# Moving one subtraction per slot of an image-token front end from VectorE to GpSimd

## The chip, the core and the metric

One core of a Trainium2 chip runs the whole program. The metric is the device time of one execution in microseconds (us), the median of several runs. Beside it stands one profiled execution, whose trace gives the start and duration of every instruction on TensorE (PE, its weight loads PEld), VectorE (DVE), ScalarE (ACT), GpSimd (POOL) and the DMA queue of SyncE (SP).

## The reference

The input is 16 images of 3 x 112 x 112, cut into 784 patches of 16 x 16. Each patch goes through a small residual network and a projection to a token of 192 numbers:

```python
x = (x - mean) / (1e-06 + std)
x = x / math.sqrt(P)
x = _conv2d(x, conv1_w, conv1_b)
residual = x
x = _group_norm(x, gn1_g, gn1_b)
x = jax.nn.gelu(x, approximate=False)
x = _conv2d(x, rconv1_w, rconv1_b)
x = _group_norm(x, gn2_g, gn2_b)
x = jax.nn.gelu(x, approximate=False)          # the second activation
x = _conv2d(x, rconv2_w, rconv2_b)
x = residual + x
x = _conv2d(x, proj_w, proj_b, stride=P, pad=0)
```

Behind it come an attention block and an MLP branch over the 16 x 49 tokens. The change doesn't touch them; they are called the tail here.

## The kernel before, in words

**Precision.** TensorE multiplies in fp16, and the kernel keeps fp32 accuracy by splitting an fp32 value into a high fp16 part and a low fp16 part, low = value - high. The first activation is split by `split1` (a cast for the high part and a subtraction for the low one, both on VectorE). The second activation, the buffer `g2f`, has its high part made by ScalarE (`hi2`) and its low part by a subtraction (`split2`, L803 to L808). Both parts go to `arena` (named `g2` in the code), where a later group's projection reads them.

**Slots.** A unit is 8 patches, a slot is 4 patches (half a unit), and there are 98 units, so 196 slots. A group is 14 units, 28 slots; there are 7 groups. In slot k TensorE runs the 3x3 convolution of slot k (15 pairs of matmuls, L501 and L502), the small matmul `means` that averages statistics over the channels of a group-norm group (L544, behind the tenth pair), and the first convolution `conv1` four slots ahead (L535, L536, behind the thirteenth pair). In groups 1 to 6 it also weaves in the projection of the group before (L556, L560), in slots 4 to 27 of the group; group 0 and the first four slots of the others have none. The last group is projected behind the loop.

**VectorE in slot k** (`slot`, L811 to L827) goes strictly in this order: four statistics of a convolution result and four of a `conv1` result (L768, eight instructions that read PSUM), `moments` (L775, L776, L778, L780: 128 x 16 elements each), `split2` of slot k-3 (L808, 128 x 512 elements), `read_means` (L784, which waits for `means` of TensorE, then L787 and L789), and `split1` of slot k+2 (L799, L801).

**GpSimd in slot k** runs `norm` (L357 to L373): it waits for L789, raises 8 variances per partition to the power -0.5 (L363) and makes scale and shift with four more instructions of 8 elements, the last being L373. ScalarE waits for the shift, and does the two Gelus (`gelu1` L417, `gelu2` L425) and `hi2` (L433).

**What sets the order.** Each engine has a program of its own, written out by hand, with loops over pairs of units and over pairs of groups, and waits on semaphores between engines. An engine never passes a waiting instruction. The semaphore `s_sp2` counts `split2`; ScalarE waits for it before it overwrites half of `g2f`, TensorE before it projects a group, and VectorE at the end. `s_sp2h` counts `hi2`.

**DMA.** SyncE issues the transfers: per slot four copies of the first activation between halves of the partitions (L276), per unit two loads of patches (L256), and chunks of projection weights (L285).

Of the kernel before, what the change touches and what calls it, by code (L numbers as in the profile page):

```python
# [20 lines left out]
ALU, ACT = mybir.AluOpType, mybir.ActivationFunctionType  # L21
# [9 lines left out]
Q = 4  # L31
UNITS = NPAT // U
GU = 14
GROUPS = UNITS // GU
# [35 lines left out]
def build_front(nc, a, emb, xs, ts, wrd):  # L70
# [9 lines left out]
    with ExitStack() as ctx:  # L80
        def sb(name, shape, dt=F32):
            return ctx.enter_context(nc.sbuf_tensor("sb_" + name, shape, dt))

        def sem(name):
            return ctx.enter_context(nc.semaphore(name))
# [6 lines left out]
        g2 = arena[:, :, :].rearrange("p b (h g n) -> p b h g n", h=2, g=G)  # L92
# [5 lines left out]
        g2f = sb("g2f", [128, U, HALF])  # L98
# [80 lines left out]
        s_g2, s_sp2h, s_sp2 = sem("gelu2_done"), sem("split2_hi"), sem("split2_done")  # L179
        s_pc, s_pj, s_pjr, s_emb = sem("chunk_used"), sem("projected"), sem("tokens_out"), sem("emb_stored")  # L180
# [7 lines left out]
        def over_groups(eng, group):  # L188

            group(0, 0, True)  # L190
            with eng.Fori(0, (GROUPS - 1) // 2) as i:
                group(2 * i + 1, 1, False)
                group(2 * i + 2, 0, False)

        def slot2(j, p, q, old):

            return (2 * GU + 2 * p + q - 3) * Q if old else j * U * 2 + (2 * p + q - 3) * Q

        def over_units(eng, g, pair, first):

            pair(g * GU, 0, first)
            with eng.Fori(1, GU // 2) as j:
                pair(g * GU + 2 * j, j, False)
# [141 lines left out]
        @block.gpsimd  # L345
        def _(pool):
            gp = nc.gpsimd
            gp.memset(half_neg[:, :], -0.5).then_inc(s_cst, 1)
            gp.memset(half_pos[:, :], 0.5).then_inc(s_cst, 1)
            gp.memset(zeros[:, :], 0.0).then_inc(s_cst, 1)  # L350
            gp.memset(zt, 0.0).then_inc(s_zero, 1)
            gp.memset(xhl.bitcast(F32), 0.0).then_inc(s_xz, 1)
            pool.wait_ge(s_cst, 3)
            pool.wait_ge(s_xvar, 1)
            gp.tensor_tensor(xsd[:, 1, :], xsd[:, 0, :], half_pos[0:ROWS, :], ALU.pow).then_inc(s_xstd, 1)

            def norm(n, s, guard=True):  # L357

                ch = Chain(pool, s_pch, n * 4)
                mean, var, (t1, t2, t3) = mst[s][:, 0, :], mst[s][:, 1, :], (tmp[s][:, k, :] for k in range(3))  # L360
                bias, gam, bet = (wid[:, k, :] for k in range(3))
                pool.wait_ge(s_rd, n + 2)
                ch.did(gp.tensor_tensor(t1, var, half_neg[:, :], ALU.pow))  # L363
                ch.did(gp.tensor_tensor(t2, mean, bias, ALU.subtract))
                pool.wait_ge(s_pch, ch.at - 1)
                if guard:
                    pool.wait_ge(s_g1, n - 1)
                    pool.wait_ge(s_g2, n - 1)
                ch.did(gp.tensor_tensor(gsc[s][:, :], t1, gam, ALU.mult))
                ch.wait()  # L370
                ch.did(gp.tensor_tensor(t3, t2, gsc[s][:, :], ALU.mult))
                ch.wait()
                gp.tensor_tensor(gsh[s][:, :], bet, t3, ALU.subtract).then_inc(s_sh, 1)  # L373

            def pair(u0, j, first):
                for p in range(2):
                    for q in range(2):
                        norm(2 * (u0 + p) + q + 3, 1 - q)

            pool.wait_ge(s_padz, 3)  # L380
            norm(0, 0, False)
            norm(1, 1, False)
            norm(2, 0)
            over_groups(pool, lambda g, b, first: over_units(pool, g, pair, first))
            norm(2 * UNITS + 3, 1)

        @block.scalar
        def _(act):
# [263 lines left out]
        def _(dve):  # L652
            v = nc.vector
# [13 lines left out]
            for src, dst in ((fst32, fws), (tst32, tws), (w1st32, w1hl)):  # L667
                hi, lo = (dst[:, k].rearrange("p a b -> p (a b)") if len(dst.shape) == 4 else dst[:, k, :] for k in range(2))
# [59 lines left out]
            for q in range(6):  # L728
                c, pr = q // 2, q % 2
                src = xt[:, c].rearrange("p w (r k j) -> p w r k j", k=2, j=P)[:, :, :, pr, :]  # L730
# [34 lines left out]
            def channel_stats(s, src, at):  # L765

                for m in range(Q):
                    v.bn_stats(bn6[s][:, at + m, :], src[:, m * HALF:(m + 1) * HALF]).then_inc(s_dch, 1)  # L768

            def moments(n, s, n0):  # L770

                ch = Chain(dve, s_dch, n0)
                ch.wait()
                b6 = bn6[s][:, :, :].rearrange("p g (e k) -> p g e k", e=2)
                ch.did(v.tensor_tensor(ms[s][:, 0, :, :], b6[:, :, :, 1], wid2[:, :, :], ALU.add))  # L775
                ch.did(v.tensor_scalar(ms[s][:, 1, :, :], b6[:, :, :, 2], 2.0 / HALF, EPS * WS * WS, ALU.mult, ALU.add))  # L776
                dve.wait_ge(s_dch, ch.at - 1)
                ch.did(v.tensor_tensor(msq[s][:, :, :], ms[s][:, 0, :, :], ms[s][:, 0, :, :], ALU.mult))  # L778
                ch.wait()
                v.tensor_tensor(ms[s][:, 1, :, :], ms[s][:, 1, :, :], msq[s][:, :, :], ALU.add).then_inc(s_ms, 1)  # L780

            def read_means(n, s):
                dve.wait_ge(s_st, n + 1)
                v.tensor_reduce(mst[s][:, :, :], st[:, 0:4 * U].rearrange("p (a b k) -> p a b k", a=2, k=2),  # L784
                                mybir.AxisListType.X, ALU.add).then_inc(s_mv, 1)
                dve.wait_ge(s_mv, 2 * n + 1)
                v.tensor_tensor(msm[s][:, :], mst[s][:, 0, :], mst[s][:, 0, :], ALU.mult).then_inc(s_mv, 1)  # L787
                dve.wait_ge(s_mv, 2 * n + 2)
                v.tensor_tensor(mst[s][:, 1, :], mst[s][:, 1, :], msm[s][:, :], ALU.subtract).then_inc(s_rd, 1)  # L789
# [10 lines left out]
                dve.wait_ge(s_sp1h, k + 1)  # L800
                v.tensor_tensor(lo, src, hi, ALU.subtract).then_inc(s_sp1, 1)  # L801

            def split2(k, q, buf, slot):  # L803

                dve.wait_ge(s_sp2h, k + 1)
                src = g2f[:, q * Q:q * Q + Q, :]
                hi, lo = (g2[:, buf, h, bass.ds(slot, Q), :] for h in range(2))
                v.tensor_tensor(lo, src, hi, ALU.subtract).then_inc(s_sp2, 1)  # L808

            def group(g, b, first):  # L810
                def slot(u, q, p, j, head, first):  # L811

                    pair_at = g * (GU // 2) + j

                    k = 2 * u + q
                    seen = not (first and p == 0 and q == 0)
                    if seen:
                        dve.wait_ge(s_rc, k)
                        channel_stats(1 - q, rc[p][0] if q == 1 else rc[1 - p][1], Q)
                    dve.wait_ge(s_c1, k + 5)  # L820
                    channel_stats(1 - q, c1[1 - q], 0)
                    moments(k + 3, 1 - q, 11 * k + 25 if seen else 25)
                    if not (first and p == 0) and not (first and p == 1 and q == 0):
                        old = head and 2 * p + q < 3
                        split2(k - 3, 1 - q, 1 - b if old else b, slot2(j, p, q, old))
                    read_means(k + 3, 1 - q)
                    split1(k + 2, q, 1 - p, pair_at + 1)  # L827

                def pair(u0, j, first, head):
                    for p in range(2):  # L830
                        for q in range(2):
                            if head and p == 1 and q == 1:
                                dve.wait_ge(s_pj, g if not first else 1)
                            slot(u0 + p, q, p, j, head, first)

                pair(g * GU, 0, first, True)
                with dve.Fori(1, GU // 2) as j:
                    pair(g * GU + 2 * j, j, False, False)
# [32 lines left out]
            K = 2 * UNITS  # L871
# [3 lines left out]
            channel_stats(1, c1[1], 0)  # L875
            moments(K + 3, 1, 11 * K + 25)
            read_means(K + 3, 1)
            for k in (K - 3, K - 2, K - 1):
                split2(k, k % 2, 0, (2 * GU + k - K) * Q)

            dve.wait_ge(s_pj, GROUPS)
            dve.wait_ge(s_sp1, K + 2)
            dve.wait_ge(s_sp2, K + 2)
# [3 lines left out]
            for c in range(C):  # L887
                for m in (2 * c, 2 * c + 1):
                    dve.wait_ge(s_tc[m % NTC], 32 * (m // NTC + 1))
                for ky in range(3):  # L890
                    for kx in range(3):
                        for py in range(2):
# [3 lines left out]
                            lo, hi = max(0, kx - 1), min(P, P + kx - 1)  # L896
# [696 lines left out]
```

## Time and profile before

| | |
|---|---|
| Device time, median of 3 runs | 1586.49 us (1581.76 to 1587.44) |
| The profiled execution | 1585.12 us, of which the span from first to last instruction is 1583.3 us |
| Granted TensorE clock, mean over the span | 0.963 |
| PE busy | 1429.4 us (90%) |
| DVE busy | 1134.6 us (72%) |
| ACT busy | 837.4 us (53%) |
| POOL busy | 581.8 us (37%) |
| The slots of the loop | from about 252 us to 1256 us of the span |

The table averages over a set-up of some 250 us, the loop and a tail of some 300 us. The limit of a stretch is read from that stretch alone: the distance between one row of a kind and the next of the same kind gives the length of a slot. A row of the timeline has the start, the duration, the engine, the line and the operation; rows of one kind that follow each other are merged, with their count.

### The profile page before, as it was taken

How to read it: one execution, taken by the hardware profiler on the slowest of the kernel's cores; microseconds unless marked ns; L12 is line 12 of the kernel's file. 1: busy time of each engine (PE TensorE's matmuls, PEld its weight loads, DVE VectorE, ACT ScalarE, POOL GpSimd, SP SyncE). 2: the span in 40 equal slices, each digit the busy share in tenths (PEclk: the TensorE clock that was granted, in tenths of full speed). 3: DMA queues.
4: the chain of work that ended last, by engine and by line, in shares of the span. 5: the costliest groups of instructions: out<-in, count | busy, mean ns of one | idle time of the engine just before them, and what ended most of it. 6: DMA issues, size and time to landing. Idle time of an engine off the chain costs nothing. (4 is left out here: it accounts for less than half of the span.)

```text
span 1583.3 us, 42709 instructions
## 1 busy us (share of the span) xinstructions
PE 1429.4 (90%) x13490; PEld 1008.6 (64%) x13490; DVE 1134.6 (72%) x4227; ACT 837.4 (53%) x2102; POOL 581.8 (37%) x1111
## 2 busy tenths in 40 slices
PE   6969996888999999989999998999999766978889
PEld 2424442333688588858877875888588666655647
DVE  7723334999988888888888887888888750474710
ACT  1212222777777676766767666666767501333442
POOL 2000003555544455444454544445554401161500
PEclk9989997999999999999999999999999887987999
DMA  6463325433555455445545553554555577300000
GB/s 181 122 205 88 99 87 220 100 101 101 138 148 143 123 150 143 131 121 145 144 119 151 146 140 101 149 147 128 139 144 143 160 202 167 71 1 1 2 3 14
DMA packets 117219, 190.63 MB, mean 120 GB/s; under 512 B 18252, under 2 KB 86284, under 8 KB 116942
## 3 DMA queue, kind: packets, MB, share of 16 engines
q1 hardware_dynamic: 117070, 188.60, 43.6%
q8 instruction: 99, 1.62, 0.4%
q14 instruction: 50, 0.41, 0.1%
HBM read 103.34 MB, written 21.30 MB: 79 GB/s over the span
## 5 line engine op out<-in xcount | busy, mean ns | idle before, releaser
L363 POOL TENSOR_TENSOR sb_tmp<-sb_mst,sb_half_neg 128x8 f32<-128x8 f32 x200 | 354.6, 1773 | 684.4 <-DVE sb_mst L789 684.4
L501 PE MATMUL rc<-sb_acts,sb_rwd 128*64 128x512 f16 x1764 | 563.5, 392 | 18.3 <-DMA sb_acts<-sb_hst 18.2
L502 PE MATMUL rc<-sb_acts,sb_rwd 128*64 128x512 f16 x1764 | 564.7, 393 | 0.0
L417 ACT ACTIVATE sb_f32q<-c,sb_gsh,sb_gsc 128x128 f32<-128x128 f32 x792 | 298.2, 458 | 285.6 <-POOL sb_gsh L373 285.6
L501 PE MATMUL rc<-sb_acts,sb_rwl 128*64 128x512 f16 x1176 | 363.9, 391 | 5.2 <-issue 5.2
L502 PE MATMUL rc<-sb_acts,sb_rwl 128*64 128x512 f16 x1176 | 363.4, 391 | 0.0
L556 PE MATMUL pj<-sb_wall,sb_arena 128*64 128x384 f16 x1792 | 309.9, 337 | 21.7 <-DMA sb_wall<-w_lo 15.1
L425 ACT ACTIVATE sb_g2f<-rc,sb_gsh,sb_gsc 128x128 f32<-128x128 f32 x784 | 297.3, 481 | 4.4 <-POOL sb_gsh L373 4.4
L560 PEld LDWEIGHTS pj<-sb_wall,sb_arena 128*64 128x64 f16 x1792 | 219.0, 222 | 63.8
L560 PE MATMUL pj<-sb_wall,sb_arena 128*64 128x192 f16 x1792 | 240.9, 247 | 0.0
L556 PEld LDWEIGHTS pj<-sb_wall,sb_arena 128*64 128x64 f16 x1792 | 215.5, 219 | 38.8 <-DMA sb_wall<-w_lo 16.4
L501 PEld LDWEIGHTS rc<-sb_acts,sb_rwd 128*64 128x64 f16 x1764 | 180.1, 110 | 79.6 <-DMA sb_acts<-sb_hst 28.4
L476 PE MATMUL rc<-sb_acts,sb_arena 128*128 128x512 f16 x864 | 196.7, 386 | 29.9 <-DVE sb_acts L684 29.9
L502 PEld LDWEIGHTS rc<-sb_acts,sb_rwd 128*64 128x64 f16 x1764 | 180.2, 110 | 4.9
L768 DVE BATCH_NORM_STATS2 sb_bn<-rc 128x6 f32<-128x128 f32 x784 | 174.0, 285 | 12.0 <-issue 5.7
L768 DVE BATCH_NORM_STATS2 sb_bn<-c 128x6 f32<-128x128 f32 x800 | 175.1, 282 | 0.5 <-PE c L536 0.5
L476 PEld LDWEIGHTS rc<-sb_acts,sb_arena 128*128 128x128 f16 x864 | 82.0, 97 | 136.2 <-issue 35.5
L501 PEld LDWEIGHTS rc<-sb_acts,sb_rwl 128*64 128x64 f16 x1176 | 126.7, 109 | 47.1 <-issue 9.6
L808 DVE TENSOR_TENSOR sb_arena<-sb_g2f,sb_arena 128x512 f32 (+1 forms) x196 | 135.7, 693 | 28.7 <-issue 18.0
L801 DVE TENSOR_TENSOR sb_acts<-sb_f32q,sb_hst 128x512 f16<-128x512 f32 x198 | 137.8, 696 | 6.8
L433 ACT ACTIVATE sb_arena<-sb_g2f 128x512 f32 (+1 forms) x196 | 124.9, 637 | 26.0 <-ACT sb_g2f L425 8.6
L502 PEld LDWEIGHTS rc<-sb_acts,sb_rwl 128*64 128x64 f16 x1176 | 126.9, 109 | 0.4 <-issue 0.3
(158 smaller groups left out, 1726.2 us busy)
## 6 DMA issues: line engine op xcount, KB each, us to landing
sb_acts<-sb_hst SPq DMA_DIRECT2D x792, 78.8 KB, 2.6
sb_wall<-w_lo SPq DMA_DIRECT2D x56, 528.0 KB, 3.8
sb_im<-x_planes SPq DMA_DIRECT2D x202, 136.5 KB
sb_wall<-w_lo SPq DMA_DIRECT2D x28, 480.0 KB, 3.7
sb_f32q<-in_proj SPq DMA_DIRECT2D x12, 576.0 KB, 3.9
sb_arena<-in_proj SPq DMA_DIRECT2D x12, 576.0 KB, 4.4
w_lo<-sb_arena SPq DMA_DIRECT2D x1, 6144.0 KB, 17.3
scratch_fold<-sb_wall SPq DMA_DIRECT2D x48, 123.8 KB
```

The source lines that it names most:

```text
L363: ch.did(gp.tensor_tensor(t1, var, half_neg[:, :], ALU.pow))
L417: ins = nc.scalar.activation(g1f[:, q * Q + m, :], c1[q][:, m * HALF:(m + 1) * HALF], ACT.Gelu, bias=gsh[q][:, m:m + 1], scale=gsc[q][:, m ...
L425: ins = nc.scalar.activation(g2f[:, q * Q + m, :], rc[p][q][:, m * HALF:(m + 1) * HALF], ACT.Gelu, bias=gsh[q][:, Q + m:Q + m + 1], scale= ...
L433: nc.scalar.activation(g2[:, buf, 0, bass.ds(slot, Q), :], g2f[:, q * Q:q * Q + Q, :], ACT.Copy).then_inc(s_sp2h, 1)
L476: last = nc.tensor.matmul(out, w[:, wp, 3 * t + m, :], v[:, xp, t:t + 8, m * Q:(m + P) * Q], start=(n == 0), stop=(n == 17))
L501: nc.tensor.matmul(out[0:CH, :], w_odd, x_odd, start=(n == 0), stop=(n == 14))
L502: yield nc.tensor.matmul(out[CH:128, :], w_even, x_even, start=(n == 0), stop=(n == 14))
L556: last = nc.tensor.matmul(pj[at:at + 64, 0:2 * E], g2[:, b, 0, k:k + 64, n], both, start=(n == 0), stop=False)
L560: last = nc.tensor.matmul(pj[at:at + 64, 0:E], g2[:, b, 1, k:k + 64, n], whi[:, n, :], start=False, stop=(n == HALF - 1))
L768: v.bn_stats(bn6[s][:, at + m, :], src[:, m * HALF:(m + 1) * HALF]).then_inc(s_dch, 1)
L801: v.tensor_tensor(lo, src, hi, ALU.subtract).then_inc(s_sp1, 1)
L808: v.tensor_tensor(lo, src, hi, ALU.subtract).then_inc(s_sp2, 1)
```

## The change

The subtraction `split2` leaves VectorE's program, where it stood between `moments` and `read_means`, and joins GpSimd's, behind `norm` of the same slot. Operands and types are the same. The wait on `s_sp2h` goes with it, and so does the wait on `s_pj` in the fourth slot of each group, which keeps a half of `arena` from being overwritten before it was projected. The last three subtractions, behind the loop, move to GpSimd too. The numbering of the semaphores stays.

```diff
-            def pair(u0, j, first):
-                for p in range(2):
-                    for q in range(2):
-                        norm(2 * (u0 + p) + q + 3, 1 - q)
+            def split2(k, q, buf, slot):
+                pool.wait_ge(s_sp2h, k + 1)
+                src = g2f[:, q * Q:q * Q + Q, :]
+                hi, lo = (g2[:, buf, h, bass.ds(slot, Q), :] for h in range(2))
+                gp.tensor_tensor(lo, src, hi, ALU.subtract).then_inc(s_sp2, 1)
+
+            def group(g, b, first):
+                def pair(u0, j, first, head):
+                    for p in range(2):
+                        for q in range(2):
+                            k = 2 * (u0 + p) + q
+                            norm(k + 3, 1 - q)
+                            if head and p == 1 and q == 1:
+                                pool.wait_ge(s_pj, g if not first else 1)
+                            if not (first and p == 0) and not (first and p == 1 and q == 0):
+                                old = head and 2 * p + q < 3
+                                split2(k - 3, 1 - q, 1 - b if old else b, slot2(j, p, q, old))
...
             norm(2 * UNITS + 3, 1)
+            for k in range(2 * UNITS - 3, 2 * UNITS):
+                split2(k, k % 2, 0, (2 * GU + k - 2 * UNITS) * Q)
...
-            def split2(k, q, buf, slot):
-
-                dve.wait_ge(s_sp2h, k + 1)
-                src = g2f[:, q * Q:q * Q + Q, :]
-                hi, lo = (g2[:, buf, h, bass.ds(slot, Q), :] for h in range(2))
-                v.tensor_tensor(lo, src, hi, ALU.subtract).then_inc(s_sp2, 1)
...
                     moments(k + 3, 1 - q, 11 * k + 25 if seen else 25)
-                    if not (first and p == 0) and not (first and p == 1 and q == 0):
-                        old = head and 2 * p + q < 3
-                        split2(k - 3, 1 - q, 1 - b if old else b, slot2(j, p, q, old))
                     read_means(k + 3, 1 - q)
                     split1(k + 2, q, 1 - p, pair_at + 1)
...
-                            if head and p == 1 and q == 1:
-                                dve.wait_ge(s_pj, g if not first else 1)
...
-            for k in (K - 3, K - 2, K - 1):
-                split2(k, k % 2, 0, (2 * GU + k - K) * Q)
```

VectorE, one slot in the body of the loop over pairs of units, from the first instruction of `moments` on, before (`sb_arena` is where the low part goes, `st` the result of `means` in PSUM; ISA and REGISTER_ALU are waits and address arithmetic):

```order
L775 TENSOR_TENSOR sb_ms<-sb_bn_0,sb_wid 128x16
L776 TENSOR_SCALAR sb_ms<-sb_bn_0 128x16
L777 REGISTER_ALU
L778 TENSOR_TENSOR sb_msq<-sb_ms 128x16
L67 REGISTER_ALU
L780 TENSOR_TENSOR sb_ms<-sb_ms,sb_msq 128x16
L805 REGISTER_ALU
L808 ISA
L808 REGISTER_ALU
L808 TENSOR_TENSOR sb_arena<-sb_g2f,sb_arena 128x512
L784 TENSOR_REDUCE sb_mst<-st 128x16
```

The same slot of the changed kernel, where the lines 775 to 784 have become 797 to 806:

```order
L797 TENSOR_TENSOR sb_ms<-sb_bn_0,sb_wid 128x16
L798 TENSOR_SCALAR sb_ms<-sb_bn_0 128x16
L799 REGISTER_ALU
L800 TENSOR_TENSOR sb_msq<-sb_ms 128x16
L67 REGISTER_ALU
L802 TENSOR_TENSOR sb_ms<-sb_ms,sb_msq 128x16
L806 TENSOR_REDUCE sb_mst<-st 128x16
```

The subtraction and its address arithmetic are gone, and the reduction that waits for TensorE's `means` stands directly behind the last instruction of `moments`.

GpSimd, one slot of the same loop, before:

```order
L363 TENSOR_TENSOR sb_tmp<-sb_mst,sb_half_neg 128x8
L364 TENSOR_TENSOR sb_tmp<-sb_mst,sb_wid 128x8
L365 ISA
L369 TENSOR_TENSOR sb_gsc<-sb_tmp,sb_wid 128x8
L67 REGISTER_ALU
L371 TENSOR_TENSOR sb_tmp<-sb_tmp,sb_gsc 128x8
L67 REGISTER_ALU
L373 TENSOR_TENSOR sb_gsh<-sb_wid,sb_tmp 128x8
L362 ISA
```

The same slot of the changed kernel:

```order
L363 TENSOR_TENSOR sb_tmp<-sb_mst,sb_half_neg 128x8
L364 TENSOR_TENSOR sb_tmp<-sb_mst,sb_wid 128x8
L365 ISA
L369 TENSOR_TENSOR sb_gsc<-sb_tmp,sb_wid 128x8
L67 REGISTER_ALU
L371 TENSOR_TENSOR sb_tmp<-sb_tmp,sb_gsc 128x8
L67 REGISTER_ALU
L373 TENSOR_TENSOR sb_gsh<-sb_wid,sb_tmp 128x8
L376 REGISTER_ALU
L379 ISA
L379 REGISTER_ALU
L379 TENSOR_TENSOR sb_arena<-sb_g2f,sb_arena 128x512
```

The subtraction, now L379, follows the shift L373 with its wait and its address arithmetic ahead of it; the next slot's wait for L789 comes behind it.

## Rows read from the trace of the kernel before

**Rows 1.** The profile's page: busy time of the engines over the whole span.

```profile
PE 1429.4 (90%) x13490; PEld 1008.6 (64%) x13490; DVE 1134.6 (72%) x4227; ACT 837.4 (53%) x2102; POOL 581.8 (37%) x1111
```

**Rows 2.** Line 789 in two stretches: count, duration (min/median/max), first and last start.

```profile
L789 DVE TENSOR_TENSOR sb_mst<-sb_mst,sb_msm x21: 166/167/170, 288.1 to 380.7; 128x8 f32<-128x8 f32 x21
...
L789 DVE TENSOR_TENSOR sb_mst<-sb_mst,sb_msm x22: 166/166/168, 412.6 to 519.3; 128x8 f32<-128x8 f32 x22
```

**Rows 3.** Stretches: length, then busy PE, PEld, DVE, ACT, POOL, clock, DMA.

```profile
288.00:385.00 97.00, 86.29 (x756) 36.34 (x756) 90.50 (x378) 73.68 (x189) 52.77 (x105) 1.00 0.40 101
410.00:522.00 112.00, 110.86 (x1256) 94.25 (x1254) 99.07 (x402) 78.20 (x199) 56.20 (x114) 1.00 0.54 146
```

**Rows 4.** Waits from 288 to 385 us: total, times, longest.

```profile
PEld st L544 <- DVE sb_ms L780: 17.8, 20, 1.0
```

**Rows 5.** Timeline of VectorE, one slot of group 0.

```profile
339.00 0.17 DVE L789 TENSOR_TENSOR sb_mst<-sb_mst,sb_msm 128x8 f32<-128x8 f32 x1
...
341.86 0.17 DVE L775 TENSOR_TENSOR sb_ms<-sb_bn,sb_wid 128x16 f32<-128x16 f32 x1
...
342.07 0.18 DVE L778 TENSOR_TENSOR sb_msq<-sb_ms 128x16 f32<-128x16 f32 x1
342.28 0.18 DVE L780 TENSOR_TENSOR sb_ms<-sb_ms,sb_msq 128x16 f32<-128x16 f32 x1
342.63 0.69 DVE L808 TENSOR_TENSOR sb_arena<-sb_g2f,sb_arena 128x512 f32 x1 [0.17 <-issue]
343.24 0.18 DVE L784 TENSOR_REDUCE sb_mst<-st 128x16 f32<-128x32 f32 x1
...
343.66 0.17 DVE L789 TENSOR_TENSOR sb_mst<-sb_mst,sb_msm 128x8 f32<-128x8 f32 x1
```

**Rows 6.** Timeline of GpSimd in the same slot, and the last step of the next.

```profile
340.97 0.20 POOL L364 TENSOR_TENSOR sb_tmp<-sb_mst,sb_wid 128x8 f32<-128x8 f32 x1
341.13 0.20 POOL L369 TENSOR_TENSOR sb_gsc<-sb_tmp,sb_wid 128x8 f32<-128x8 f32 x1
...
341.68 0.20 POOL L373 TENSOR_TENSOR sb_gsh<-sb_wid,sb_tmp 128x8 f32<-128x8 f32 x1
...
346.47 0.20 POOL L373 TENSOR_TENSOR sb_gsh<-sb_wid,sb_tmp 128x8 f32<-128x8 f32 x1
```

**Rows 7.** Timeline of VectorE behind the last slot, where no subtraction stands between.

```profile
1254.68 0.17 DVE L780 TENSOR_TENSOR sb_ms<-sb_ms,sb_msq 128x16 f32<-128x16 f32 x1
1255.27 0.19 DVE L784 TENSOR_REDUCE sb_mst<-st 128x16 f32<-128x32 f32 x1 [0.41 <-PE st L544]
1255.50 0.17 DVE L787 TENSOR_TENSOR sb_msm<-sb_mst 128x8 f32<-128x8 f32 x1
1255.70 0.17 DVE L789 TENSOR_TENSOR sb_mst<-sb_mst,sb_msm 128x8 f32<-128x8 f32 x1
```

**Rows 8.** Timeline of a slot with projection: GpSimd, then VectorE.

```profile
706.56 0.20 POOL L373 TENSOR_TENSOR sb_gsh<-sb_wid,sb_tmp 128x8 f32<-128x8 f32 x1
...
706.86 0.18 DVE L778 TENSOR_TENSOR sb_msq<-sb_ms 128x16 f32<-128x16 f32 x1
707.07 0.17 DVE L780 TENSOR_TENSOR sb_ms<-sb_ms,sb_msq 128x16 f32<-128x16 f32 x1
```

**Rows 9.** Timelines of VectorE and GpSimd where their instructions overlap, or don't.

```profile
257.61 0.69 DVE L801 TENSOR_TENSOR sb_acts<-sb_f32q,sb_hst 128x512 f16<-128x512 f32 x1
...
257.71 0.65 POOL L371 TENSOR_TENSOR sb_tmp<-sb_tmp,sb_gsc 128x8 f32<-128x8 f32 x1
...
1406.29 0.84 DVE L1433 TENSOR_TENSOR tl_pr<-tl_pr,tl_mx 128x294 f32<-128x294 f32 x2
...
1417.27 1.36 DVE L1433 TENSOR_TENSOR tl_pr<-tl_pr,tl_mx 128x294 f32<-128x294 f32 x2
...
1416.61 1.32 POOL L1071 TENSOR_TENSOR tl_kb<-tl_big,tl_hmask 96x294 f32<-96x294 f32 x2
```

**Rows 10.** GpSimd on two tensors of 294 elements, in the tail: duration min/median/max.

```profile
L1071 POOL TENSOR_TENSOR tl_kb<-tl_big,tl_hmask x64: 672/678/905, 1384.9 to 1496.1; 96x294 f32<-96x294 f32 x64
```

**Rows 11.** SyncE's queue of transfers in group 0.

```profile
341.96 1.56 SPq L256 DMA_DIRECT2D sb_im<-x_planes  x2
344.23 7.03 SPq L276 DMA_DIRECT2D sb_acts<-sb_hst  x8
```

More of the change, by code:

```diff
@@ L373, in norm @@
                 gp.tensor_tensor(gsh[s][:, :], bet, t3, ALU.subtract).then_inc(s_sh, 1)
-            def pair(u0, j, first):
-                for p in range(2):
-                    for q in range(2):
-                        norm(2 * (u0 + p) + q + 3, 1 - q)
+            def split2(k, q, buf, slot):
[14 more added lines that the diff above has]
+                                split2(k - 3, 1 - q, 1 - b if old else b, slot2(j, p, q, old))
+                pair(g * GU, 0, first, True)
+                with pool.Fori(1, GU // 2) as j:
+                    pair(g * GU + 2 * j, j, False, False)
             pool.wait_ge(s_padz, 3)
@@ L383, in _ @@
             norm(2, 0)
-            over_groups(pool, lambda g, b, first: over_units(pool, g, pair, first))
+            group(0, 0, True)
+            with pool.Fori(0, (GROUPS - 1) // 2) as i:
+                group(2 * i + 1, 1, False)
+                group(2 * i + 2, 0, False)
             norm(2 * UNITS + 3, 1)
+            for k in range(2 * UNITS - 3, 2 * UNITS):
+                split2(k, k % 2, 0, (2 * GU + k - 2 * UNITS) * Q)
         @block.scalar
```

## The prediction

> **What bounds the kernel now.** The page comes first, and it misleads: PE is busy for 90% of the span, VectorE for 72%, GpSimd for 37% [rows 1]. That reads as if GpSimd had plenty of room for one more subtraction. Shares over the span mix a set-up, a loop and a tail, and the change touches the loop alone, so I went on to the length of a slot there. L789 comes once in each slot. In group 0, which has no projection, 21 of them start between 288.1 and 380.7 us: 92.6 over 20 intervals, 4.63 us a slot. With projection, 22 start between 412.6 and 519.3: 106.7 over 21, 5.08 us a slot [rows 2]. Two kinds of slot, and the busy time of the stretches tells their limits: with projection PE is busy for 110.86 of 112 us; without it for 86.29 of 97, and it waits for VectorE's L780, 20 times, 17.8 us by the weight loads [rows 3, 4]. The third view is VectorE's timeline in such a plain slot: its instructions follow each other without a hole from one L789 to the next [rows 5] (starts overlap by some 0.1 us, so that 90.50 busy of 97 is a full engine). So plain slots are bound by VectorE's order, slots with projection by PE, and GpSimd idles in both.
>
> **What the change removes.** VectorE loses the 0.69 us subtraction L808 in each slot, but not all of its time is won. Before, L780 ends at 342.28 + 0.18 = 342.46 and L784 starts at 343.24, 0.78 us later [rows 5]. L784 needs TensorE's `means`, which needs L780; the subtraction lay over that round trip. Where nothing stands between, behind the last slot, L780 ends at 1254.85 and L784 starts at 1255.27, having waited for PE: 0.42 us [rows 7]. So the removal is worth 0.78 - 0.42 = 0.36 us in a plain slot, and nothing in a slot that PE bounds.
>
> **What it adds on GpSimd.** 196 subtractions of 128 x 512. No row has GpSimd at this size, so bounds: L1071 takes 0.678 us for 294 elements [rows 10], an instruction of 8 elements 0.20 [rows 6]. A straight line through both gives 0.20 + 0.478 x 504 / 286 = 1.04 us, simple proportion 0.678 x 512 / 294 = 1.18. I take 1.12, the middle; the two differ little. Its input is ready: the high part of slot k-3 is made a whole slot before GpSimd gets there, so the moved wait costs nothing, and neither does that on `s_pj`, whose projection ended at least three slots before. Queued behind the subtraction on GpSimd is only the next `norm`, which waits for the next L789. That leaves it room: L373 starts 2.68 or 2.81 us behind L789 (341.68 - 339.00, 346.47 - 343.66) [rows 5, 6], mean 2.75; with dispatch and 1.12 the engine is free before 4.3. No transfer is moved. ScalarE, which waits for `s_sp2` before it refills half of `g2f`, does a Gelu of its own first. By throughput the change is free.
>
> **What it costs: a collision.** VectorE and GpSimd get in each other's way here, and rows of this trace price it. VectorE's pair of L1433, each reading two tensors in SBUF, takes 0.84 us when GpSimd is quiet; started at 1417.27, while GpSimd's L1071 runs until 1416.61 + 1.32 = 1417.93, the pair takes 1.36: 0.52 longer, which is what was left of GpSimd's instruction (0.66) less some 0.14 [rows 9]. It goes the other way too: L371 of GpSimd, 0.20 us elsewhere, takes 0.65 when it starts under L801 and ends just behind it (257.71 + 0.65 = 258.36 against 258.30) [rows 9]. An instruction that reads SBUF on the one engine holds off one that reads two SBUF tensors on the other until it ends.
>
> Now lay the new subtraction on the timeline. It starts behind L373 by its dispatch: 0.16 us from L364 to L369, where a wait stands between (341.13 - 340.97) [rows 6], or 0.35 from L780 to L808, where address arithmetic and a wait do (342.63 - 342.28) [rows 5]. The order shows both on GpSimd now, so 0.35: it starts at 342.03. VectorE's L778 is due at 342.07 and L780 at 342.28 [rows 5]; in a slot with projection L373 starts at 706.56, the subtraction would at 706.91, L778 is due at 706.86 and L780 at 707.07 [rows 8]. So GpSimd gets in ahead of L780, and often of L778. Both read two SBUF tensors. They wait for its end, `means` waits for L780, L784 for `means`, L789 for L784, and GpSimd's next `norm` for L789: the wait closes a ring of its own. From L789 to the next L789:
>
> - to L373: 2.75; dispatch 0.35; subtraction 1.12;
> - release to the end of L780: 0.03 (its 0.18 less the 0.15 seen above);
> - L780 to L784: 0.42 [rows 7]; L784 to L789: 0.43 (1255.70 - 1255.27) [rows 7].
>
> That is 5.10 us if L780 alone is caught. If L778 is, L780 starts 0.21 behind it (342.28 - 342.07) [rows 5]: 5.31. It is nearly a tie between them, so I take the mean, 5.20 us for every slot. This is above VectorE's 4.63 and above PE's 5.08.
>
> The sum: 25 plain slots of group 0 at 5.20 - 4.63 = 0.57 give 14 us. 144 slots with projection (6 groups x 24) at 5.20 - 5.08 = 0.12 give 17. The 24 slots at the heads of groups 1 to 6 have waits of their own mixed in; I count half of a plain one's loss, an estimate: 7. Behind the loop the last three subtractions stand behind the last `norm`, and the last Gelu needs the half of `g2f` that the first of them frees: 1.12, and the last is longer by 1.12 - 0.69: 1.6 us. Together 40. The profiled execution took 1585.1 us (span 1583.3), 1.4 below the median of the runs: 1585 + 40 = 1625 us. With L780 alone caught, 12 + 6 + 3 + 2 = 22, 1607 us; with L778 always, 17 + 8 + 33 + 2 = 60, 1645 us; with the bounds of the subtraction's price some 4 to 10 us further out on either side. So 1600 to 1655 for this case by itself.
>
> The Trainium skill, SBUF — State Buffer, section Who interferes with whom, says that a VectorE instruction with two SBUF inputs contends with a GpSimd instruction that reads SBUF, and that whoever starts first keeps the shared ports for the whole instruction while the other is fully blocked. The rows above agree, but for 0.14 us of VectorE's start that the block hides. By the page alone each slot would be longer by that much, 0.15 us, and the sum 1652 instead of 1625.
>
> **The rivals.** *GpSimd comes too late.* If dispatch takes over 0.51 to 0.60 us (707.07 - 706.56, 342.28 - 341.68) [rows 5, 6, 8], L780 gets in first. It starts 3.28 behind L789, ends at 3.46, the subtraction runs from there to 4.58 and catches L787, due at 3.46 + 0.42 + 0.23 = 4.11 (L787 starts 0.23 behind L784 [rows 7]). That is held to about 4.43, and L789 comes at 4.63: the plain slot as before, PE's slot as before, and the end's 1.6 us: 1587. For it: the margin is 0.2 us, less than dispatch is known to.
>
> *No collision for small reads.* VectorE's instructions of 16 elements might slip through. Then plain slots gain 0.36, down to 4.27, but SyncE issues 7.03 + 1.56 us of transfers in two slots, 4.30 each [rows 11]: 0.33 x 25 = 8 us, 4 at the heads, and at best the 1% that PE idles with projection (1.14 of 112 [rows 3]), 7 of 731 us. Less 1.6, 1567 us, on the other side of no change. It decides if L780 ends less than 0.78 - 0.42 = 0.36 us later than it does now. Against it: GpSimd's block in rows 9 came for an instruction of 8 elements.
>
> *A dearer subtraction.* If mixed fp32 and fp16 operands cost GpSimd 1.6 us, each slot gains another 0.48: 1712 us or so. Nothing speaks for it but that no row has these types on GpSimd.
>
> **How the numbers follow.** The collision gets 0.60, GpSimd too late 0.18, no collision 0.12, the dearer subtraction 0.10. I forecast the likeliest, 1625 us. The range goes from 1570, just above the full gain, to 1668, above the page's case; outside it lie most of the dear case and a few of the hundredths of the gain. A measurement of this kernel tells 0.5% (8 us) from no change. Collision and dear price are slower by more: 0.70. Too late is the same: 0.18. No collision is faster: 0.12.
>
> **What would show it.** In the changed kernel's trace: GpSimd's subtraction at 1.04 to 1.18 us, starting 0.3 to 0.4 behind the shift; VectorE's second or third product of `moments` (128 x 16, 0.18 before) stretched to about 1 us in most slots; L789's successor every 5.1 to 5.3 us in all groups alike; PE waiting for `moments` with projection too, where it hardly did. Wrong would be: those instructions still at 0.18, or a subtraction that starts behind them, or one of over 1.3 us. Plain slots of 4.3 us would be the second rival.

## The result, and the profile after

The changed kernel takes 1643.59 us (median of 4 runs, 1640.66 to 1644.95), the kernel before 1584.85 us in the same comparison (median of 4, 1581.76 to 1587.44): 1.0369 times as long, 95% interval 1.0343 to 1.0395. Slower, as forecast, by 59 us where 40 were forecast; the time lies inside the range of 1570 to 1668.

Its page answers to [rows 1]:

```profile
PE 1454.5 (89%) x13490; PEld 984.6 (60%) x13490; DVE 1174.1 (72%) x4031; ACT 838.8 (51%) x2102; POOL 810.2 (49%) x1307
```

VectorE lost 196 instructions of 0.69 us, 135 us in all, and is busy for 40 us *more* than before. That is the first sign: its other instructions have become longer. The line that closes a slot, now L811, shows where the time went. First over the whole run, in the kernel before and then in the one after (count, duration min/median/max, first and last start):

```profile
L789 DVE TENSOR_TENSOR sb_mst<-sb_mst,sb_msm x200: 166/166/173, 252.7 to 1255.7; 128x8 f32<-128x8 f32 x100
```

```profile
L811 DVE TENSOR_TENSOR sb_mst<-sb_mst,sb_msm x200: 166/166/176, 252.7 to 1312.1; 128x8 f32<-128x8 f32 x100
```

The set-up ends at the same time, 252.7. The loop has grown from 1003.0 to 1059.4, by 56.4 us; the span has grown by 1641.7 - 1583.3 = 58.4, so 2.0 remain for what stands behind the loop. The same line in group 0 and in group 1, which answers to [rows 2]:

```profile
L811 DVE TENSOR_TENSOR sb_mst<-sb_mst,sb_msm x19: 166/166/169, 304.5 to 398.0; 128x8 f32<-128x8 f32 x19
...
L811 DVE TENSOR_TENSOR sb_mst<-sb_mst,sb_msm x21: 166/166/174, 429.4 to 536.1; 128x8 f32<-128x8 f32 x21
```

A plain slot takes 93.5 / 18 = 5.19 us (4.63 before), a slot with projection 106.7 / 20 = 5.33 (5.08 before). The busy times and the waits of these stretches, for [rows 3, 4]:

```profile
300.00:399.00 99.00, 75.04 (x692) 35.87 (x689) 87.94 (x324) 67.14 (x172) 70.28 (x115) 1.00 0.35 90
425.00:540.00 115.00, 111.83 (x1221) 86.52 (x1218) 101.71 (x369) 75.77 (x193) 80.39 (x132) 1.00 0.50 136
```

```profile
PEld st L566 <- DVE sb_ms L802: 33.2, 19, 1.9
...
PEld st L566 <- DVE sb_ms L802: 9.2, 21, 1.8
```

The first wait is that of group 0: 33.2 us in 19 slots where there were 17.8 in 20. The second is from the slots with projection: TensorE, which bounded them, now waits there for `moments` as well, 9.2 us by the weight loads in 115. In the kernel before, the same wait from 410 to 522 us was this:

```profile
PEld st L544 <- DVE sb_ms L780: 0.8, 1, 0.8
```

In both kinds of slot it is now a ring of waits that sets the length, and no engine by itself. VectorE and then GpSimd in one plain slot, for [rows 5, 6]:

```profile
351.30 0.17 DVE L811 TENSOR_TENSOR sb_mst<-sb_mst,sb_msm 128x8 f32<-128x8 f32 x1
...
354.40 0.17 DVE L800 TENSOR_TENSOR sb_msq<-sb_ms 128x16 f32<-128x16 f32 x1
354.61 1.01 DVE L802 TENSOR_TENSOR sb_ms<-sb_ms,sb_msq 128x16 f32<-128x16 f32 x1
356.03 0.19 DVE L806 TENSOR_REDUCE sb_mst<-st 128x16 f32<-128x32 f32 x1 [0.41 <-PE st L566]
...
356.46 0.17 DVE L811 TENSOR_TENSOR sb_mst<-sb_mst,sb_msm 128x8 f32<-128x8 f32 x1
```

```profile
354.11 0.20 POOL L373 TENSOR_TENSOR sb_gsh<-sb_wid,sb_tmp 128x8 f32<-128x8 f32 x1
354.41 1.18 POOL L379 TENSOR_TENSOR sb_arena<-sb_g2f,sb_arena 128x512 f32 x1
```

The whole ring is to be read off: 2.81 us from L811 to the shift, 0.30 to the subtraction, 1.18 for it until 355.59, 0.03 to the end of L802 at 355.62, 0.41 for TensorE's `means`, 0.43 to the next L811. That makes 5.16. The last product of `moments`, 0.18 us by itself, was issued 0.2 us behind the subtraction and lasted until its end.

A slot with projection looks like this on VectorE, then on GpSimd, and at the end of a convolution on TensorE:

```profile
482.72 0.17 DVE L811 TENSOR_TENSOR sb_mst<-sb_mst,sb_msm 128x8 f32<-128x8 f32 x1
...
483.26 0.69 DVE L823 TENSOR_TENSOR sb_acts<-sb_f32q,sb_hst 128x512 f16<-128x512 f32 x1
484.07 0.89 DVE L790 BATCH_NORM_STATS2 sb_bn<-rc 128x6 f32<-128x128 f32 x4
...
485.78 1.12 DVE L797 TENSOR_TENSOR sb_ms<-sb_bn,sb_wid 128x16 f32<-128x16 f32 x1
...
488.16 0.17 DVE L811 TENSOR_TENSOR sb_mst<-sb_mst,sb_msm 128x8 f32<-128x8 f32 x1
```

```profile
485.41 0.20 POOL L373 TENSOR_TENSOR sb_gsh<-sb_wid,sb_tmp 128x8 f32<-128x8 f32 x1
485.69 1.17 POOL L379 TENSOR_TENSOR sb_arena<-sb_g2f,sb_arena 128x512 f32 x1
```

```profile
483.65 0.38 PE L524 MATMUL rc<-sb_acts,sb_rwd 128*64 128x512 f16 x1
```

Here the statistics L790 begin 0.81 us behind L823 (352.48 - 351.87 = 0.61 in the plain slot), since the convolution that they read isn't ready sooner: its last matmul ends at 484.03 as the profile models it, 0.04 us ahead of L790. `moments` is later by the same 0.2 us, and the subtraction gets in ahead of its *first* instruction. The other three follow only then, and the slot is 5.44 us long. The four lines of `moments` and the subtraction over the whole run:

```profile
L797 DVE TENSOR_TENSOR sb_ms<-sb_bn,sb_wid x200: 174/179/1187, 250.3 to 1310.5; 128x16 f32<-128x16 f32 x100
...
L798 DVE TENSOR_SCALAR sb_ms<-sb_bn x200: 152/166/1193, 250.4 to 1310.8; 128x16 f32<-128x16 f32 x100
...
L800 DVE TENSOR_TENSOR sb_msq<-sb_ms x200: 159/175/1211, 250.5 to 1310.9; 128x16 f32<-128x16 f32 x100
...
L802 DVE TENSOR_TENSOR sb_ms<-sb_ms,sb_msq x200: 174/175/1161, 250.8 to 1311.1; 128x16 f32<-128x16 f32 x100
...
L379 POOL TENSOR_TENSOR sb_arena<-sb_g2f,sb_arena x196: 1151/1178/1245, 286.4 to 1318.3; 128x512 f32 x168, 128x512 f16<-128x512 f32 x28
```

All medians are below 0.2 us and all maxima at 1.2: in a slot one of the four is caught, and not always the same. A group's mean or median would hide this; the maximum and the timeline show it. Counted in the timeline by which of the four lasted over 0.45 us:

| Caught | Group 0, 300 to 399 us: slots, mean length | 425 to 1300 us: slots, mean length |
|---|---|---|
| L797, the first | 0 | 59, 5.42 |
| L798, the second | 5, 5.21 | 17, 5.30 |
| L800, the third | 6, 5.24 | 32, 5.32 |
| L802, the fourth | 7, 5.15 | 48, 5.21 |

The longer stretch holds the four heads, without projection, of groups 2 to 6 as well, and six of its 162 slots have none of that length. Between 425 and 1300 us the statistics begin 0.78 us behind L823 on average in the 59 slots of the first row, 0.62 to 0.64 in the other rows.

### The profile page after: what moved, and what is told of

Same layout as the page of the kernel before. It is cut to its first block and busy times, and to the rows that moved or that the text cites. A ratio compares the mean times of both kernels' runs of the same rounds, so it can differ in the third digit from the quotient of the medians.

```text
span 1641.7 us, 42709 instructions
## 1 busy us (share of the span) xinstructions
PE 1454.5 (89%) x13490; PEld 984.6 (60%) x13490; DVE 1174.1 (72%) x4031; ACT 838.8 (51%) x2102; POOL 810.2 (49%) x1307
## 5 line engine op out<-in xcount | busy, mean ns | idle before, releaser
L578 PE MATMUL pj<-sb_wall,sb_arena 128*64 128x384 f16 x1792 | 300.6, 337 | 20.7 <-DMA sb_wall<-w_lo 12.8
L582 PEld LDWEIGHTS pj<-sb_wall,sb_arena 128*64 128x64 f16 x1792 | 212.3, 226 | 74.0
L379 POOL TENSOR_TENSOR sb_arena<-sb_g2f,sb_arena 128x512 f32 (+1 forms) x196 | 231.7, 1183 | 16.1 <-issue 2.9
L578 PEld LDWEIGHTS pj<-sb_wall,sb_arena 128*64 128x64 f16 x1792 | 209.3, 222 | 40.7 <-DMA sb_wall<-w_lo 14.4
L582 PE MATMUL pj<-sb_wall,sb_arena 128*64 128x192 f16 x1792 | 231.3, 247 | 0.0
L790 DVE BATCH_NORM_STATS2 sb_bn<-rc 128x6 f32<-128x128 f32 x784 | 173.7, 283 | 11.5 <-issue 5.5
L790 DVE BATCH_NORM_STATS2 sb_bn<-c 128x6 f32<-128x128 f32 x800 | 174.3, 278 | 0.5 <-PE c L558 0.5
L523 PEld LDWEIGHTS rc<-sb_acts,sb_rwl 128*64 128x64 f16 x1176 | 126.6, 109 | 49.2 <-issue 7.7
L823 DVE TENSOR_TENSOR sb_acts<-sb_f32q,sb_hst 128x512 f16<-128x512 f32 x198 | 137.9, 696 | 6.8
L566 PE MATMUL st<-sb_ms,sb_grp 128*64 128x32 f32 x800 | 62.1, 234 | 74.0 <-DVE sb_ms L802 63.1
```

Of the source, the lines that this page charges most:

```text
L379: gp.tensor_tensor(lo, src, hi, ALU.subtract).then_inc(s_sp2, 1)
L523: nc.tensor.matmul(out[0:CH, :], w_odd, x_odd, start=(n == 0), stop=(n == 14))
L578: last = nc.tensor.matmul(pj[at:at + 64, 0:2 * E], g2[:, b, 0, k:k + 64, n], both, start=(n == 0), stop=False)
L582: last = nc.tensor.matmul(pj[at:at + 64, 0:E], g2[:, b, 1, k:k + 64, n], whi[:, n, :], start=False, stop=(n == HALF - 1))
```

## The experiments

Six kernels beside the two. Each is compared with the kernel before on the same chip (1586.0 us, for the last two 1585.56).

**1. The ceiling.** The kernel before, and VectorE's subtraction is left out: the low part of the second activation is not formed, and memory that is then written by nothing is zeroed once in the set-up. What is left is the most that any place for the subtraction could give.

```diff
-                v.tensor_tensor(lo, src, hi, ALU.subtract).then_inc(s_sp2, 1)
+                v.sem_inc(s_sp2, 1)
```

> The kernel before, with the subtraction left out on VectorE and put nowhere else (the low part of the second activation is never formed; its semaphore is still counted there; 1 us of zeroing is added ahead of the loop). This prices the removal alone. Collision theory: removing is worth something, plain slots 4.27 to 4.35 us instead of 4.63, slots with projection 5.05 to 5.08, time 1567 to 1576 us. Rival (the move loses because VectorE now waits for TensorE's means with nothing to cover the round trip): 1585 us or more.

Measured: 1581.69 us, 0.9974 times (0.9957 to 0.9991). The end of a slot (now L795) over the whole run, in plain slots, and with projection, then SyncE's queue in group 0:

```profile
L795 DVE TENSOR_TENSOR sb_mst<-sb_mst,sb_msm x200: 166/166/175, 256.9 to 1254.7; 128x8 f32<-128x8 f32 x100
...
L795 DVE TENSOR_TENSOR sb_mst<-sb_mst,sb_msm x19: 166/166/168, 301.5 to 381.6; 128x8 f32<-128x8 f32 x19
...
L795 DVE TENSOR_TENSOR sb_mst<-sb_mst,sb_msm x19: 166/166/168, 426.5 to 517.4; 128x8 f32<-128x8 f32 x19
```

```profile
335.80 1.56 SPq L257 DMA_DIRECT2D sb_im<-x_planes  x2
337.80 6.94 SPq L277 DMA_DIRECT2D sb_acts<-sb_hst  x8
344.78 1.56 SPq L257 DMA_DIRECT2D sb_im<-x_planes  x2
```

A plain slot takes 80.1 / 18 = 4.45 us, not 4.3, and a slot with projection 90.9 / 18 = 5.05. So the expectation missed: without 135 us of VectorE's work the time is 4 us shorter. Not all of the difference is the subtraction's: the loop starts at 256.9 us here and at 251.6 to 253.2 in the six profiles without the zeroing (252.7 in the kernel before), so that some 4 us of the experiment's time are its own set-up. The loop itself takes 1254.7 - 256.9 = 997.8 us for 1003.0. Less that set-up the time would be about 1577 us, an estimate, and the work is worth some 8 us, 0.5%. SyncE issues for 8.50 us of the 8.98 between its two rows of L257, two slots; what closes the rest of that ring wasn't taken apart. With the rest of the kernel as it is, no place for the subtraction can gain more than about this 0.5%.

**2. The collision alone.** The kernel before keeps its subtraction on VectorE; GpSimd gets one more of the same size behind each `norm`, on fp16 constants, and nothing waits for it.

```diff
                         norm(2 * (u0 + p) + q + 3, 1 - q)
+                        gp.tensor_tensor(junk[:, :], rwl[:, 0:8, :].rearrange("p a b -> p (a b)"),
+                                         rwd[:, 0:8, :].rearrange("p a b -> p (a b)"), ALU.subtract)
```

> The kernel before, subtraction left on VectorE, and on GpSimd behind each norm a further 128x512 subtraction of two constant weight tensors in SBUF into an unused tensor, which nobody waits for. This adds the collision alone, without moving any dependence. Collision theory: an instruction of moments is stretched by about 1 us in nearly every slot, the ring is 2.75 + 0.3 + 1.18 + 0.03 + 0.78 + 0.43 = 5.47 us, time 1650 to 1680 us. Rival (the move loses by the changed order of waits: what waits for the subtraction gets it later): 1585 to 1590 us.

Measured: 1701.16 us, 1.0741 times (1.0717 to 1.0766). Slots are 78.4 / 14 = 5.60 us without projection and 89.7 / 16 = 5.61 with it. One slot, GpSimd and then VectorE:

```profile
343.46 0.20 POOL L374 TENSOR_TENSOR sb_gsh<-sb_wid,sb_tmp 128x8 f32<-128x8 f32 x1
343.62 1.15 POOL L380 TENSOR_TENSOR sb_junk<-sb_rwl,sb_rwd 128x512 f16<-128x512 f16 x1
```

```profile
343.64 1.16 DVE L778 TENSOR_TENSOR sb_ms<-sb_bn,sb_wid 128x16 f32<-128x16 f32 x1
344.73 0.16 DVE L779 TENSOR_SCALAR sb_ms<-sb_bn 128x16 f32<-128x16 f32 x1
...
345.38 0.69 DVE L811 TENSOR_TENSOR sb_arena<-sb_g2f,sb_arena 128x512 f32 x1 [0.16 <-issue]
```

Work that no one waits for, in time in which its engine was idle, costs 115 us. That is the collision by itself. It is larger than expected for a reason that these rows show too: this subtraction has fixed addresses and no wait, starts 0.16 us behind the shift rather than 0.30, and so catches the first instruction of `moments` more often (for over 0.45 us in 101 slots of the whole run, 61 in the changed kernel), and then all four come later; the fourth is never caught in this run. When the block comes decides its price as much as how long it is.

**3. A write in place of a read.** The same place in the kernel before, but GpSimd only writes: a memset of 128 x 780 fp16, 0.75 us.

```diff
                         norm(2 * (u0 + p) + q + 3, 1 - q)
+                        gp.memset(junk[:, :], 0.0)
```

> The kernel before, and on GpSimd behind each norm a memset of 128x780 fp16 into an unused tensor, about 0.72 us, at the place of the further subtraction of extra_read. It occupies GpSimd and reads nothing. Collision through reads: no instruction of moments is stretched, 1583 to 1590 us. Rival (any GpSimd instruction holds VectorE off, or a longer GpSimd program is what costs): the ring is 2.75 + 0.3 + 0.72 + 0.03 + 0.78 + 0.43 = 5.01 us in plain slots, 1595 to 1605 us.

Measured: 1600.26 us, 1.0103 times (1.0076 to 1.013). The time is the rival's, but the rows tell another story than either: GpSimd, then VectorE.

```profile
345.74 0.75 POOL L380 MEMSET sb_junk<- 128x780 f16 x1
```

```profile
345.78 0.17 DVE L777 TENSOR_TENSOR sb_ms<-sb_bn,sb_wid 128x16 f32<-128x16 f32 x1
345.87 0.65 DVE L778 TENSOR_SCALAR sb_ms<-sb_bn 128x16 f32<-128x16 f32 x1
345.99 0.53 DVE L780 TENSOR_TENSOR sb_msq<-sb_ms 128x16 f32<-128x16 f32 x1
346.57 0.17 DVE L782 TENSOR_TENSOR sb_ms<-sb_ms,sb_msq 128x16 f32<-128x16 f32 x1
...
L777 DVE TENSOR_TENSOR sb_ms<-sb_bn,sb_wid x200: 174/176/205, 250.0 to 1265.7; 128x16 f32<-128x16 f32 x100
...
L778 DVE TENSOR_SCALAR sb_ms<-sb_bn x200: 165/650/756, 250.0 to 1265.8; 128x16 f32<-128x16 f32 x100
```

L777, with two tensors in SBUF, is never held (0.205 us at most in 200), though the memset is running when it starts in 97 of them; L778, with one, is held until the memset ends. L780 stands behind it on VectorE: in the five slots in which L778 started ahead of the memset and L780 under it (the first at 311.5 us), L780 took 0.17 us. So what holds the two-tensor instructions is that GpSimd *reads*, as the prediction had it; but a `tensor_scalar` is held by a GpSimd instruction that reads nothing, which the prediction had left out. The Trainium skill, SBUF — State Buffer, section Who interferes with whom, says both: two SBUF inputs contend only with a GpSimd instruction that reads SBUF, while `tensor_scalar` can enter a mode that takes the shared ports for itself and so contends with any. This trace agrees, with 0.17 us for L777 and 0.65 for L778; that L778 ran in such a mode is not itself seen in it.

**4. Another moment.** The changed kernel, with the subtraction held until the next slot's `moments` is done.

```diff
                 pool.wait_ge(s_sp2h, k + 1)
+                pool.wait_ge(s_ms, min(k + 8, 2 * UNITS + 4) if isinstance(k, int) else k + 8)
```

> The changed kernel with one more wait on GpSimd: the subtraction starts only when VectorE's moments of the next slot are done. Same instructions, same work, a later start. Collision theory: moments are at 0.17 us each again, the second instruction of read_means is held instead by 0.2 to 0.5 us, plain slots 4.6 to 4.7 us, 1583 to 1595 us. Rival (GpSimd is simply too slow for this subtraction, or its later result is what is waited for): 1640 us or more, since the result comes later still.

Measured: 1597.84 us, 1.0088 times (1.0055 to 1.0122); of the changed kernel's 3.7% some 0.9% are left, and `moments` is never held. But the block has moved on. VectorE, then GpSimd, in group 0:

```profile
340.45 0.17 DVE L803 TENSOR_TENSOR sb_ms<-sb_ms,sb_msq 128x16 f32<-128x16 f32 x1
341.04 0.19 DVE L807 TENSOR_REDUCE sb_mst<-st 128x16 f32<-128x32 f32 x1 [0.41 <-PE st L567]
341.26 0.89 DVE L810 TENSOR_TENSOR sb_msm<-sb_mst 128x8 f32<-128x8 f32 x1
```

```profile
340.97 1.16 POOL L380 TENSOR_TENSOR sb_arena<-sb_g2f,sb_arena 128x512 f32 x1 [0.81 <-DVE sb_ms L803]
```

The subtraction starts 0.35 us after the end of the instruction that it waited for (340.62 to 340.97), so that little of its 1.16 us lies under the round trip of `means`, which is over at 341.04. L807, which reads PSUM, passes; L810, which reads SBUF twice, is held until 342.15. Plain slots take 80.0 / 16 = 5.00 us, slots with projection 91.5 / 18 = 5.08, as in the kernel before. My expectation was a little too low, since it had the subtraction start at once.

**5. Half the length.** The changed kernel, with GpSimd forming only the first two of each slot's four patches (the rest of the low part is zero, from a memset in the set-up).

```diff
-                gp.tensor_tensor(lo, src, hi, ALU.subtract).then_inc(s_sp2, 1)
+                gp.tensor_tensor(lo[:, 0:2, :], src[:, 0:2, :], hi[:, 0:2, :], ALU.subtract).then_inc(s_sp2, 1)
```

> The changed kernel with half of the subtraction: GpSimd forms the low part for 2 of the 4 patches of each slot (128x256 elements), the other half is never formed; 1 us of zeroing is added ahead of the loop. Collision theory: the block is as long as what is left of GpSimd's instruction, so about 0.68 us instead of 1.18, the ring 0.5 us shorter: 4.6 to 5.0 us by which instruction is caught, mean 4.8 in plain slots, slots with projection back at PE's 5.08; 1587 to 1598 us. Rival (the move costs by its order of waits, whatever the length): 1625 us or more.

Measured: 1594.86 us, 1.0049 times (1.003 to 1.0068). The instruction, by the page (busy us, then mean ns), and the longest that any line of `moments` took, here its third:

```profile
L383 POOL TENSOR_TENSOR sb_arena<-sb_g2f,sb_arena 128x256 f32 (+1 forms) x196 | 133.6, 682 | 15.0 <-ACT sb_arena L459 1.7
```

```profile
L806 DVE TENSOR_TENSOR sb_msq<-sb_ms x200: 159/176/720, 254.2 to 1263.9; 128x16 f32<-128x16 f32 x100
```

The held instruction is as long as the shorter block, 0.72 us at most, and plain slots fall to 80.6 / 17 = 4.74 us, slots with projection to 91.3 / 18 = 5.07. Half the block costs 0.5% rather than 3.7%, and some 4 of these 9 us are again the zeroing in the set-up (the first L817 starts at 256.4 us). With projection nothing is lost: where the ring of waits isn't longer than what bounds the slot, the block costs no time.

**6. The same work in four pieces.** The changed kernel, with the whole subtraction as four instructions of 128 x 128.

```diff
-                hi, lo = (g2[:, buf, h, bass.ds(slot, Q), :] for h in range(2))
-                gp.tensor_tensor(lo, src, hi, ALU.subtract).then_inc(s_sp2, 1)
+                for m in range(Q):
+                    hi, lo = (g2[:, buf, h, bass.ds(slot + m, 1), :] for h in range(2))
+                    ins = gp.tensor_tensor(lo, src[:, m:m + 1, :], hi, ALU.subtract)
+                ins.then_inc(s_sp2, 1)
```

> The changed kernel with the same subtraction cut into four instructions of 128x128 elements on GpSimd, back to back, about 0.4 us from one to the next. Collision theory: VectorE gets in between two of them, each of its instructions on two SBUF tensors waits for the end of one quarter only, ring 4.8 to 5.15 us, 1592 to 1615 us although GpSimd is busy longer (1.6 us). Rival (what counts is when the whole subtraction ends, or how busy GpSimd is): 1660 us or more, since it ends 0.4 us later.

Measured: 1589.89 us, 1.0027 times (1.001 to 1.0044). GpSimd and VectorE in one slot, then the page's row of the pieces:

```profile
342.98 1.60 POOL L380 TENSOR_TENSOR sb_arena<-sb_g2f,sb_arena 128x128 f32 x4
```

```profile
343.04 0.40 DVE L800 TENSOR_SCALAR sb_ms<-sb_bn 128x16 f32<-128x16 f32 x1
343.36 0.17 DVE L802 TENSOR_TENSOR sb_msq<-sb_ms 128x16 f32<-128x16 f32 x1
343.56 0.29 DVE L804 TENSOR_TENSOR sb_ms<-sb_ms,sb_msq 128x16 f32<-128x16 f32 x1
...
L380 POOL TENSOR_TENSOR sb_arena<-sb_g2f,sb_arena 128x128 f32 (+1 forms) x784 | 316.3, 433 | 13.4 <-ACT sb_arena L457 0.8
```

GpSimd now works 1.60 us per slot for what took it 1.18, and yet the ratio falls from 1.0369 to 1.0027, a little below what was expected. Plain slots take 79.0 / 17 = 4.65 us, slots with projection 91.0 / 18 = 5.06. VectorE's short instructions get in between two pieces. Of the two readings of the slow-down, that GpSimd has too much to do or that one long instruction holds VectorE off, only the second survives this. It is still no gain over the kernel before, where the first experiment leaves room for 0.5% at most.

## Why the prediction was right, and where its sizes were off

**The mechanism is shown.** The work added alone, with nothing waiting for it, makes the loss (experiment 2); moving it off `moments` (4), halving it (5) or cutting it up (6) removes most of it. Of the rivals, GpSimd too late (1587) and no collision (1567) fall by the rows of L797 to L802, and the dearer subtraction by L379's 1.18 us, which is the upper bound that the prediction gave for 1.12. Dispatch was 0.30 us in the plain slot shown and 0.22 to 0.32 in 150 of the 196 slots, for 0.35. The end of the held instruction, 0.03 us behind the release, was as taken. The case by the Trainium skill alone had 0.15 us more per slot, and 1652; the measured time is nearer to that than to 1625, but not for its reason: in the rows above the 0.15 us are hidden.

**The terms of the sum.** Plain slots: 25 x (5.19 - 4.63) = 14 us, forecast 14. That they agree so well is partly chance: the shorter dispatch and the longer subtraction, 0.05 and 0.06 us, cancel, and the second instruction is caught there too. Behind the loop 2.0 us for 1.6, which says little: that stretch is 327.6 us in the kernel before and 329.7 in experiment 3, which ends in the same way. Slots with projection: the 144 of them take 764.6 us from L811 to L811, and 730.7 from L789 to L789 before, 34 us more (5.31 a slot for 5.07), forecast 17. The heads of groups 1 to 6, summed in the same way, take 9 us more, forecast 7. The mis-sized term is that of the projection, and the step is "I take the mean, 5.20 us for every slot": it allowed only L778 or L780 of the old numbering to be caught, the third and the fourth, with 5.31 as its longest. Measured between 425 and 1300 us, the first is caught in 59 of 156 slots, at 5.42, and the second in 17. Two things had been left out. `moments` comes later there against GpSimd's chain, because the statistics wait for TensorE, which is the busy engine in those slots: in 47 of the 53 slots with projection in which the first is caught, they begin 0.80 us or a little more behind L823, and 0.04 behind the end of the convolution's last matmul. And the second instruction, a `tensor_scalar` with one SBUF tensor, was taken as one that can't be held. That it can be is seen in the table above and, without any GpSimd read, in experiment 3.

**The removal.** Worth "0.36 us in a plain slot" by the round trip; experiment 1 has 4.63 - 4.45 = 0.18. This didn't enter the sum, since the collision overrides it, but the rival that ends on the other side was priced with it: without any subtraction the kernel takes 1581.69 us, some 1577 less the added set-up, so 1567 could not have been reached even with no collision.

## What to carry to other kernels

An idle engine isn't a free one: before moving work from VectorE to GpSimd, lay the new instruction on the timeline and look which VectorE instructions on the ring of waits read SBUF while it runs, since even one of 16 elements is held to its end. If the work has to be there, cut it into several short instructions, or put it under instructions that read PSUM (seen for L807 of experiment 4 alone, and not tried for a whole subtraction), and allow for the start behind a wait (0.35 us here). And time the kernel with the work left out first: here that shows that 135 us of busy time was worth some 8, and the set-up that such a run adds has to be taken off.

## What the runs showed of the hardware that was not expected

A GpSimd memset, which reads nothing, holds a `tensor_scalar` of 128 x 16 on VectorE for as long as it runs (0.65 us in the median for 0.17), and doesn't hold a `tensor_tensor` with two SBUF inputs beside it (0.176). GpSimd's subtraction takes 1.18 us for 512 elements, 0.68 for 256 and 0.43 for 128, which lies on a line of 0.18 us and 1.95 ns an element (worked out from the three); four of the shortest in a row take 1.60, 0.13 less than four times 0.43, since their rows overlap (the next starts about 0.39 us behind the last). A subtraction of 512 elements starts 0.16 us behind the start of its predecessor when its addresses are fixed, whether there is no wait (experiment 2) or one already met (26 of the 28 such slots of the changed kernel); with address arithmetic and the wait already met it is 0.22 to 0.32 in 150 of 168 slots. Behind a wait that has just been met, it starts 0.35 us after the end of the instruction waited for (experiment 4).
